# A graph network on one core: the first aggregation's dense sums over two PSUM banks, and what shares a bank with what

## The reference

```python
h = jnp.maximum(_layernorm(x), 0.0)
# layer 0: weighted neighbour sum, one product with W1, leaky relu
m_j = norm[:, None] * (x_j + x_j * x_i @ W1_w.T + W1_b)
x = x + leaky(segment_sum(m_j, to_, n))
h = jnp.maximum(_layernorm(x), 0.0)
# layer 1: twice: mean over neighbours
mean_neigh = segment_sum(h[src], dst, n) / max(deg, 1)
h = h @ W_self.T + mean_neigh @ W_neigh.T + b      # relu between the two
x = x + h
```

## Time and profile before

| | us |
|---|---|
| median of three runs | 3341.88 |
| lowest, highest | 3338.53, 3342.33 |
| the profiled execution | 3346.14 |
| its span, first to last instruction | 3344.1 |
| TensorE busy | 2979.4 (89%) |
| TensorE's weight loads | 2602.2 (78%) |
| GpSimd busy | 2237.0 (67%) |
| VectorE busy | 1935.4 (58%) |
| ScalarE busy | 1322.4 (40%) |

### The profile page before, as it was taken

How to read it: one execution, slowest core, us unless ns; L and a number is a source line. 1 busy time by engine, 2 the same in 40 slices (tenths; PEclk the granted TensorE clock), 3 DMA queues, 4 the chain that set the end, 5 groups by cost and what they waited for, 6 DMA issues and landing times.

```text
span 3344.1 us, 73461 instructions
## 1 busy us (share of the span) xinstructions
PE 2979.4 (89%) x27729; PEld 2602.2 (78%) x27729; DVE 1935.4 (58%) x5525; ACT 1322.4 (40%) x3331; POOL 2237.0 (67%) x2220
## 2 busy tenths in 40 slices
PE   1068788899998898989899999999999999999998
PEld 0046577688787787878788888888888888888888
DVE  6689999999898898989354444432221221222221
ACT  1324566687787787878244444421110000000000
POOL 7716765677777777777366665666664777677673
PEclk9999999999999999999999999999999999999999
DMA  7362344455455455545566666676665666666664
GB/s 213 96 123 79 105 121 120 125 152 158 140 164 151 139 151 164 158 138 150 160 202 221 219 196 212 219 238 195 215 201 166 215 221 219 209 209 211 215 216 153
DMA packets 479015, 581.78 MB, mean 174 GB/s; under 512 B 62620, under 2 KB 443265, under 8 KB 478169
## 3 DMA queue, kind: packets, MB, share of 16 engines
q1 hardware_dynamic: 352132, 404.43, 37.6%
q0 software_dynamic: 69168, 145.24, 16.6%
q10 hardware_dynamic: 57360, 27.34, 3.0%
HBM read 412.81 MB, written 164.77 MB: 173 GB/s over the span
## 4 chain that ended last, share of the span: by engine, by line
PE 59%; POOL 17%; DVE 16%; issue 7%; DMA 1%; ACT 1%; ACTq 0%; DVEq 0%; POOLq 0%
PE ps L1670 48%; POOL arena L1445 13%; DVE arena L1975 6%; DVE arena L1970 5%; PE ps L1581 4%; PE ps L1640 4%; POOL arena L1414 3%; PE ps L1616 2%; DMA arena<-parts,arena 1%; DVE arena L1989 1%; PE ps L1606 0%; POOL arena L1422 0%; DVE arena L2042 0%; DVE arena L2076 0%; DVE arena L2082 0%
## 5 line engine op out<-in xcount | busy, mean ns | idle before, releaser
L1445 POOL DMA_INDIRECT arena<-parts,arena x1991 | 2058.5, 1034 | 836.0 <-issue 573.1
L1670 PE MATMUL ps<-arena 128*128 128x256 f16 (+2 forms) x18816 | 2469.1, 274 | 65.1 <-DVEq L2043 58.0
L1670 PEld LDWEIGHTS ps<-arena 128*128 128x128 fp8e3 x18816 | 1805.2, 98 | 285.1 <-ACT arena L1237 59.6
L1237 ACT ACTIVATE arena<-ps 128x392 fp8e3<-128x392 f32 x2176 | 1048.9, 500 | 630.5 <-PE ps L1640 588.2
L1640 PE MATMUL ps<-arena 128*128 128x196 bf16 (+1 forms) x5806 | 786.7, 241 | 76.2 <-DVE arena L1975 66.5
L1640 PEld LDWEIGHTS ps<-arena 128*128 128x128 bf16 x5806 | 500.3, 101 | 189.5 <-DVE arena L1975 78.7
L1975 DVE TENSOR_TENSOR arena<-arena 128x1176 bf16<-128x1176 bf16 (+6 forms) x1016 | 644.7, 635 | 0.0
L1989 DVE TENSOR_TENSOR arena<-arena 128x256 bf16<-128x256 bf16 x864 | 232.7, 314 | 700.0 <-PE ps L1581 696.3
L1970 DVE TENSOR_TENSOR arena<-arena 128x768 bf16<-128x768 bf16 (+5 forms) x1016 | 539.8, 531 | 105.7 <-PE ps L1640 91.1
L1581 PE MATMUL ps<-arena 128*128 128x256 f16 (+1 forms) x1991 | 291.8, 275 | 39.4 <-DMA arena<-parts,arena 38.9
L2058 DVE SCALAR_TENSOR_TENSOR arena<-ps,rdegs,arena 128x128 f32<-128x128 f32 x196 | 68.6, 350 | 382.5 <-PE ps L1670 350.7
(11 more groups left out here) (192 smaller groups left out, 1142.1 us busy)
## 6 DMA issues: line engine op xcount, KB each, us to landing
arena<-counts SPq DMA_DIRECT2D x132, 1568.0 KB
counts<-arena SPq DMA_DIRECT2D x68, 1568.0 KB
arena<-parts,arena POOLq DMA_INDIRECT x1991
arena<-table SPq DMA_DIRECT2D x294, 64.0 KB
arena<-parts SPq DMA_DIRECT2D x28, 448.0 KB, 5.0
parts<-arena ACTq DMA_DIRECT2D x108, 64.0 KB
table<-arena ACTq DMA_DIRECT2D x108, 64.0 KB
parts<-arena SPq DMA_DIRECT2D x14, 455.0 KB, 9.5
```

What stands on the lines that cost most here:

```text
L1237: act.activation(to, ps[:, unit_bank(q), 0:(b - a) * tiles].rearrange("p (n a) -> p a n", n=b - a), ACT.Copy, saturate=False).then_inc(s_e ...
L1445: pool.indirect_dma_start(to, None, parts_of[nth], bass.IndirectOffsetOnAxis(ap=tail_idx[:, i, first + c:first + c + 1], axis=0)).then_inc ...
L1670: m = pe.matmul(bank(b, 0, w), stage[k][:, a, :], rows_in[nth][:, a, 0:w], start=e == 0, stop=e == tiles - 1, skip_group_check=True)
```

## The change

- Dense sums of the first aggregation use bank 2 up to step 4, and from step 5 on banks 6 and 2 in turn; a product waits for the `take` of the last sum in its own bank.
- For batches after the last one with several visits (batch 5 after the change), destinations and sources are both turned into the upper half of bank 4, beside `u` in its first quarter. VectorE then makes the low keys too, as a copy right behind the keys; ScalarE's `lows` stay for batches up to 5. `turn_u` waits for key and low of the records.
- `h` is transposed into the last quarter of bank 7 in the first aggregation, beside `y` and the W1 product, with the waits that keep ScalarE's and VectorE's reads apart from TensorE's writes.
- ScalarE's `turned_u` moves from 42% and 88% of a group to 27% and 66%.
- The planner breaks off before a batch of pairs with more than one visit, behind group 4: groups 14 and 15 become two batches of single nodes. Before there were 43 batches, 1016 groups of one-hots and 5806 visits; now 44, 1012 and 5891.

```diff
+DENSE_BANKS = (2, 6)
...
@@ plan_batches
                 vs = [visits_of(g * P + i * n, n, n_nodes, n_edges) for i in range(P)]
+                if n > 1 and vs[0] > 1 and g > 4:
+                    break
                 c = best[g] + sum(vs) * (0.085 + 0.1 * n) + 6.0
...
+    last_deep = max(k for k in range(batches_to[0]) if deepest[k] > 1)
+    dense_banks, before_in_bank = [], []
+    for g in range(GROUPS):
+        dense_banks.append(DENSE_BANKS[g % 2] if g > batches[last_deep][0] // P + 1 else DENSE_BANKS[0])
+        before_in_bank.append(max((p for p in range(g) if dense_banks[p] == dense_banks[g]), default=None))
...
+        def dst_columns(k, j, n):
+            return bank(4, 2 * P + j, 2 * P + j + n) if last_deep < k < batches_to[0] else bank(4, j, j + n)
+        def src_columns(k, j, n):
+            return bank(4, 3 * P + j, 3 * P + j + n) if last_deep < k < batches_to[0] else bank(6, j, j + n)
+        def h_bank(nth):
+            return bank(7, 3 * P, 4 * P) if nth == 0 else bank(6, 0, P)
...
@@ turned_h (ScalarE)
                     act.wait_ge(s_hps, n + 1)
-                    if n >= 2:
+                    if nth == 0:
+                        act.wait_ge(s_y, n)
+                    elif n >= 2:
                         act.wait_ge(s_y, n - 1)
-                    act.activation(hT[:, r % 2, :], bank(6, 0, P), ACT.Copy).then_inc(s_hT, 1)
+                    act.activation(hT[:, r % 2, :], h_bank(nth), ACT.Copy).then_inc(s_hT, 1)
...
-                        now = [round(len(here) * part / 100) for part in (0, 8, 42, 46, 50, 54, 60, 88, 92, 96)]
+                        now = [round(len(here) * part / 100) for part in (0, 8, 27, 46, 50, 54, 60, 66, 92, 96)]
...
-                        if i == 0 and 1 <= b < batches_to[0] - 1:
+                        if i == 0 and 1 <= b < last_deep:
                             lows(b + 1)
...
@@ w1_product (TensorE)
                     pe.wait_ge(s_yS, y_out[0])
+                    pe.wait_ge(s_hT, turned_out[1])
                     pe.matmul(w1_bank(j), uT[:, r % 2, :], w_t[:, 0, :], start=True, stop=True).then_inc(s_w1, 1)
...
@@ small_products (TensorE)
-                    pe.wait_ge(s_low, records_out[0])
-                    pe.transpose(bank(6, 0, P), h[:, r % 2, :], ident[:, :]).then_inc(s_hps, 1)
+                    if nth == 0:
+                        pe.wait_ge(s_yS, y_out[0])
+                        pe.wait_ge(s_w1free, w1_out[0])
+                    else:
+                        pe.wait_ge(s_low, records_out[0])
+                    pe.transpose(h_bank(nth), h[:, r % 2, :], ident[:, :]).then_inc(s_hps, 1)
...
                     pe.wait_ge(s_w1free, w1_out[0])
+                    if nth == 0 and turned_out[1] == n + 1:
+                        pe.wait_ge(s_hT, n + 1)
...
@@ product (TensorE)
-                b = 2 if nth == 0 else (steps_before[nth] + s) % 2
+                b = dense_bank(nth, s)
...
+                        elif before_in_bank[s] is not None:
+                            pe.wait_ge(s_free, before_in_bank[s] + 1)
                         else:
-                            pe.wait_ge(s_free, s)
+                            pe.wait_ge(s_low, last_deep + 1)
...
@@ keys_of (VectorE)
+                if last_deep < k < batches_to[0]:
+                    dve.tensor_copy(low_of(k)[:, 0:m, :], src_columns(k, 0, m).unsqueeze(2).to_broadcast([P, m, 2])).then_inc(s_low, 1)
```

16 lines of the change are left out of this document (9 added, 7 removed).

## The result

The changed kernel takes **3367.27 us** (median of 4, 3360.28 to 3369.43) against 3341.81 us for the kernel before (3338.53 to 3342.33): ratio 1.0075, 95% interval 1.0057 to 1.0092. That is 25 us slower, where 3337 was forecast with 3350 as the upper end. The profiled execution took 3366.75 us, its span is 3362.5. Outside the span lie 4.2 us, before 2.0: 2.2 us of the difference are in no row of the trace.

What follows compares the result with a forecast made beforehand. VectorE was taken to bound the deep stretch, GpSimd's full gather queue the paired one, TensorE and VectorE the last. Terms +1.6 - 1.1 - 2.4 - 3.5 + 0.5 = -4.9 us from 3341.88 gave 3337 us, range 3326 to 3350.

Steps and rivals of the forecast that it cites:

- signs of being wrong: Wrong if gathers leave 1.1 us, group 14 starts outside 643-652 us, or last-stretch TensorE waits at `u` over 2 us per batch.
- The deep stretch, +3.5: Groups 6 to 13: stalls gone -3.4, copies on VectorE +4.4, waits around `u` +2.5; +3.5 us at group 14's start.
- -3.4 credited for stalls gone: Deep stretch: three quarters of VectorE's 4.6 us of waiting for TensorE was to go, -3.4 us.
- Rival 3: Deep stretch: VectorE pays for copies and the held `u`, GpSimd carries the delay on; +8.3, 3350 us, chance 12%.
- Groups 14 and 15, +1.6 and -1.1: GpSimd's restart 2.8 us later with a `land` of 1.25 done, +1.6; 19 gathers beside single-batch one-hots cheaper, -1.1 us.
- a `land` "already done": Groups 14 and 15: one `land` of 1.25 us was counted as finished before GpSimd's gathers restart at 677.1.
- The paired stretch, -2.4: Groups 16 to 50: only stalls behind GpSimd's own waits for TensorE pay, -2.4 us; copies and `land` order hidden.
- Rival 5: Paired stretch: each of 17 VectorE copies holds a gather for 0.43 us; +2.4, 3344.3 us, chance 4%.
- waits for gathers (+30 us): Paired stretch: TensorE's stalls at the dense product were to return as some 30 us more waiting for gathers.
- The last stretch, -3.5: Groups 51 to 55, bound shared by TensorE and VectorE: 0.6 of TensorE's 5.9 us of stalls go, -3.5 us.
- Bank 7, +0.5: `h` beside `y` and the W1 product costs only in the first aggregation's closing ticks: +0.5 us, bounds 0 and +3.
- the cover that I named: Bank 7's added waits were to be hidden, as groups last 21 us and these steps lie a quarter group apart.

Runs made afterwards that it cites:

- e12: Kernel before with only `turned_u` moved to 27% and 66% of a group: 3341.68 us, ratio 0.9999.
- e13: The changed kernel run again, unchanged, for a second profiled execution: 3362.97 us, ratio 1.0061.
- e1: Kernel before plus only the planner's break (groups 14 and 15 as two single batches): 3346.16 us, ratio 1.0010.
- e6: Kernel before plus planner's break and VectorE copying the low keys, records left in their old bank: 3353.88 us, ratio 1.0037.
- e3: The changed kernel without the planner's break, so groups 14 and 15 stay one batch of pairs: 3360.45 us, ratio 1.0050.
- e9: The changed kernel with `turned_u` back at 42% and 88% of a group, two banks still in turn: 3363.57 us, ratio 1.0062.
- e10: Kernel before plus planner's break, VectorE's low-key copy, records beside `u` with its waits, and `h` in bank 7; dense sums all in bank 2: 3362.23 us, ratio 1.0050.
- e17: The changed kernel with seven visits per one-hot group instead of six and keys two groups sooner: 3338.15 us, ratio 0.9989.
- e8: Kernel before with only the next batch's keys made two groups of one-hots sooner: 3349.75 us, ratio 1.0032.
- e14: Kernel before with seven visits of pairs per one-hot group instead of six: 3355.65 us, ratio 1.0059.
- e15: Kernel before with eight visits of pairs per one-hot group instead of six: 3360.07 us, ratio 1.0060.
- e7: e6 plus records in bank 4 beside `u`, which waits for key and low key: 3350.16 us, ratio 1.0027.
- e11: e7 plus `turned_u` at 27% and 66% of a group: 3353.32 us, ratio 1.0038.
- e16: The changed kernel with seven visits per one-hot group instead of six: 3354.62 us, ratio 1.0039.
- e18: The changed kernel with seven visits per one-hot group and without the planner's break: 3348.17 us, ratio 1.0025.
- e2: The changed kernel with all dense sums in bank 2, the alternation undone: 3363.41 us, ratio 1.0063.
- e4: The changed kernel with the next batch's keys and low keys two groups of one-hots sooner: 3355.80 us, ratio 1.0044.
- e5: e1 plus `h` in bank 7 with that place's waits: 3346.77 us, ratio 1.0020.

## Why the prediction was wrong

**Held.** That GpSimd is full in the paired stretch; that the stalls of L1706 vanish; that the second half of the run stays as it is; that GpSimd loses its 17.9 us of idling at 674 (it idles 19.26 us at the `land` of 649.64 instead) and shows no block over 1 us; the price of the copy, 0.41 us against 0.4 taken; `turned_u`'s moments at 0 in the kernel before (e12). Of the signs of being wrong, two came: gathers changed from 1115 ns (1122 and 1134), and group 14 starts at 653.1, after 652, in the first profile (649.6 in e13).

**The deep stretch, +3.5.** The sum came out about right, but not by its terms, so that was luck: at the start of group 14 after and e13 are 7.0 and 3.5 us behind before, 3.7 and 3.2 of it already at group 6. The copies cost what they were charged (e1 against e6). Of the -3.4 credited for stalls gone, at most 1.9 came: VectorE waited 4.6 us for TensorE before, 5.4 in after and 2.7 in e13, while 13.1 us at `u` took the stalls' place in both. Rival 3, with its 12%, was the nearest in time and named the wait at `u`, but it put the whole loss into this stretch and stopped at 3350. e3, which has none of it here and is 17 to 18 us slower, speaks against that.

**Groups 14 and 15, +1.6 and -1.1.** The restart was forecast at 677.1 and came at 680.3, of which 3.7 were already there at group 6: the sum for the restart itself was right. But I then credited 1.25 us for a `land` "already done". The planner's break adds a batch, so the same number of `land`s remains behind it: the credit was an error of counting. The 19 gathers of group 16, which were to be 0.06 us cheaper each, show no gain: 1.155 us on average before, 1.201 in after and 1.173 in e13. e1 prices the whole reshuffle at +3 us, interval 0 to 6.

**The paired stretch, -2.4: the step that failed worst.** The blocks did go (5.1 to 1.5 us). I then wrote that the copies, the `land` order and all other shifts "are hidden by GpSimd", taking its 1.115 us per gather as fixed. It is not: 1085 to 1134 ns over the kernels here, 26 us between the ends for 523 gathers. Groups 16 to 49 were to take 2.4 us less and took 4.3 (e13) to 5.0 us (after) more, with 8.0 us more of GpSimd's own operations in both. Rival 5 held a part of this (VectorE slows gathers) but tied it to the copy. The rows say otherwise: the gather below begins 0.13 us ahead of the copy of 797.99 and runs over it, and takes 0.94 us. The 18 gathers of after and e13 that begin 0.11 or 0.12 us ahead of a copy take no more than 0.95.

```profile
797.86 0.94 POOL L1471 DMA_INDIRECT arena<-parts,arena  x1 [0.31 <-issue]
```

I also had TensorE's freed time go to waits for gathers (+30 us); against before they grew by 8.2, and e9 and e10 show +5 there and +21 at `u` and `h`.

**The last stretch, -3.5.** The dense stalls are gone, but VectorE's waits for TensorE are not (1479 to 1608; 11.1 in the earlier trace rows), and GpSimd, late as it now is, is waited for once more at the end:

```profile
DVE arena L2008 <- PE ps L1674: 12.2, 6, 5.7
...
PE ps L1607 <- DMA arena<-parts,arena: 4.1, 3, 2.8
```

From group 51 to 56 it is 107.1 us instead of 103.5 (1501.3 to 1608.4, 1488.7 to 1592.2), 105.1 in e13, 106.9 in e9 and 103.8 in e10: with two banks and six visits it is shorter in none of them. Which wait decides it there was not told apart.

**Bank 7, +0.5.** Right place, size off: 2 to 4 us, the upper bound of 3 or just over it. In the paired stretch the cover that I named was gone too once the alternation had TensorE close behind VectorE (6.5 us at L1637).

**Outside the span, 0.** Not thought of: 2.2 us, cause open.

By the ratios: planner 3, copy and records 6, `h` with them 8, alternation 4, moments 0 to 4. Each has an interval of about 4 us either way, and after and e13 themselves differ by 4. So the split over the parts is rough. That making room costs more than the second bank gives, with the old constants, is shown (e10 alone is 12 to 22 us above before, and e9 is not below it); why just this order of VectorE's list holds more gathers than the old one is not.

## What to carry to other kernels

When a wait is removed from an engine that does not set the pace, read what it will reach next on the engine that does, and price that wait from the edit's own extra conditions; here they were the price of the room for the second buffer, and came to more than the buffer could give. A mean duration in a profile is no constant: before taking a full queue's time per item as fixed, look at its spread and at what runs when the long ones begin and when they end. Here the ends told it: those of all long gathers but one lay 0.82 us behind the end of a one-hot on another engine. And where two engines run in step, one size of a group or one place in a list can be worth as much as the structural change (here 8 to 20 us, with either sign), so try these constants again after each such change, on the old kernel too.

## What was not expected of the hardware

An indirect gather of this size takes 0.94 us on GpSimd when it is not held, and 1.1 to 1.7 us when a one-hot of VectorE (two bf16 inputs, both in SBUF) runs some 0.12 us behind its start: it then ends 0.82 us after a one-hot does. Behind two one-hots and more it can take longer (2.80 us in after). The other operations of VectorE in the eight profiles, over the same stretch, sort themselves by the number and the place of their inputs. The short ones with two inputs in SBUF, f32 and f16, hold a gather too, until their own end, and it mostly stays at or below 1.09 us. Those with an operand in PSUM do not hold it (310 gathers, 0.94 or 0.95 us), so it is not VectorE's being busy that does it. Of those with one input, out of SBUF, BATCH_NORM_STATS2 does not (87 gathers, 0.94 or 0.95), TENSOR_SCALAR does (4 gathers, 0.97 to 0.99). What goes beyond 0.944 us a gather adds up, over groups 16 to 49, to 89 us before, 93 and 98 in after and e13, and 74 in e17; the mean of a kernel moves by over 4% (1085 to 1134 ns) with the order, length and place of the one-hots. All of this is read from the traces; no run took the one-hots away or moved their inputs.

The Trainium skill ("SBUF - State Buffer", "Who interferes with whom" and its list of operations that take the shared port pair) says that a `tensor_tensor` with both inputs in SBUF contends with GpSimd's reads, which agrees, and infers that it leaves descriptor generation alone. The traces do not speak against that inference: the 0.82 us behind the hold run under one-hots without getting longer. Which part of a gather does what they do not show.

The time outside the span differs from kernel to kernel and is mostly the same in all executions of one: 2.0 to 2.4 us in every run of before, 2.0 to 2.5 in e8, e14 and e15, 1.7 to 1.9 in e3, e6, e7, e11, e16, e17 and e18, 3.6 to 4.6 in after, e2, e4, e9, e10 and e13. It is not quite fixed: e5 has 1.9 to 3.4, e1 1.7 to 1.8 and once 2.7, e12 2.0 to 2.2 and once 2.9.
